# Two small VectorE operations, the clamp of the sums of squares and the layer norms' epsilon, are done on GpSimd beside its powers

## The reference, cut to what matters

```
x = x + 0.5 * ffn(layernorm(x))
x = x + attention(layernorm(x))          # 16 heads of 8, causal
x = x + 0.5 * ffn(layernorm(x))

def ffn(x):                              # 2 layers, 8 heads of 64, window 64
    for l in range(2):
        h = shift_token(x);  q, k, v = split(h @ wqkv[l])
        q = q / max(|q|, 1e-12) * q_scale;  k = k / max(|k|, 1e-12) * k_scale
        q, k = rotary_xpos(q, k)
        x = x + local_attention(q, k, v) @ wo[l]
        h = shift_token(x);  h = (h - mean) / sqrt(var + 1e-5) * ln_g + ln_b
        a, g = split(h @ w1[l] + b1[l]);  x = x + (a * gelu(g)) @ w2[l] + b2[l]
```

## Time and profile before

| | |
|---|---|
| median of 3 runs | 2004.96 us (2004.87 to 2005.1) |
| the profiled execution's own time | 2005.93 us |
| its span in the trace | 2004.1 us |
| busy: PE, DVE, ACT, POOL | 1722.5, 1670.6, 1584.0, 1202.8 us |
| granted TensorE clock, mean | 0.963 of full speed |
| HBM read and written | 5.91 and 2.10 MB |

### The profile page before, as it was taken

One profiled execution on the slowest core, in us unless ns is written; L12 is line 12 of the kernel. 1 busy time (PEld: TensorE's weight loads), 2 busy tenths in 40 slices (PEclk: granted clock), 3 DMA queues, 4 the chain that ended last, 5 costly groups with the idle time before them and its releaser, 6 DMA issues.

```text
span 2004.1 us, 48536 instructions
## 1 busy us (share of the span) xinstructions
PE 1722.5 (86%) x17528; PEld 1353.8 (68%) x17528; DVE 1670.6 (83%) x3487; ACT 1584.0 (79%) x4960; POOL 1202.8 (60%) x1162
## 2 busy tenths in 40 slices
PE   3688999898788899888888889988878889988986
PEld 2477776677667676677766777667766767666775
DVE  6688887888888887888899887888988897888884
ACT  2468897878786899888877789888868778988874
POOL 7677304687678801577788850366767791066870
PEclk7799998999999999999999999999999999999998
DMA  3100000010110000000011000000100010000000
GB/s 100 25 20 12 10 1 17 10 23 20 25 28 20 18 1 3 15 18 18 23 33 25 18 9 1 9 17 17 23 17 23 17 26 2 1 17 18 18 18 11
DMA packets 31686, 36.29 MB, mean 18 GB/s; under 512 B 7986, under 2 KB 18652, under 8 KB 31452
## 3 DMA queue, kind: packets, MB, share of 16 engines
q1 hardware_dynamic: 31452, 33.19, 7.2%
HBM read 5.91 MB, written 2.10 MB: 4 GB/s over the span
## 4 chain that ended last, share of the span: by engine, by line
DVE 36%; ACT 28%; PE 17%; issue 10%; POOL 9%; DMA 0%; ACTq 0%; POOLq 0%; DVEq 0%
ACT probs L885 13%; DVE parts L1152 10%; PE ps_pool L1224 5%; DVE sums L1157 5%; DVE probs L1073 5%; ACT turned L903 4%; POOL rnorm L821 3%; DVE neg_max L1060 3%; PE ps_pool L1297 3%; POOL parts L818 3%; POOL roped L827 3%; ACT L885 2%; ACT L950 2%; DVE sums_floor L1160 2%; PE ps_pool L1368 2%
## 5 line engine op out<-in xcount | busy, mean ns | idle before, releaser
L885 ACT ACTIVATE probs<-ps_scores,neg_max 128x128 f32<-128x128 f32 (+1 forms) x1536 | 577.5, 412 | 71.6 <-DVE neg_max L1060 70.0
L818 POOL TENSOR_TENSOR parts<-parts 128x256 f32<-128x256 f32 x512 | 392.1, 787 | 331.1 <-DVE parts L1152 331.1
L821 POOL TENSOR_TENSOR rnorm<-sums_floor,neg_half 128x8 f32<-128x8 f32 x256 | 440.3, 1720 | 0.0
L885 ACT ACTIVATION_READ_ACCUMULATOR probs<-ps_scores,neg_max 128x1 f32 x1536 | 358.5, 234 | 0.0
L1152 DVE TENSOR_TENSOR parts<-ps_pool,rope 128x1024 f32<-128x1024 f32 x256 | 311.5, 1217 | 38.6 <-ACT squares L931 33.0
L806 POOL TENSOR_TENSOR rstd<-var_eps,neg_half 128x2 f32<-128x2 f32 x112 | 82.0, 732 | 416.8 <-DVE var_eps L1088 413.6
L1060 DVE TENSOR_REDUCE neg_max<-ps_scores 128x4 f32<-128x512 f32 (+1 forms) x448 | 295.4, 682 | 27.5 <-PE ps_scores L1265 16.7
L827 POOL TENSOR_TENSOR roped<-parts,rnorm 128x512 f32<-128x512 f32 x256 | 294.9, 1152 | 37.2 <-POOL rnorm L821 0.9
L1297 PE MATMUL ps_pool<-ident,probs 128*128 128x128 f32 x1792 | 265.7, 286 | 56.0 <-DVE probs L1073 34.8
L903 ACT ACTIVATE turned<-ps_pool 128x512 f32<-128x512 f32 x448 | 255.6, 617 | 63.9 <-PE ps_pool L1297 62.9
L1073 DVE TENSOR_TENSOR probs<-probs,prob_inv 128x1024 f32<-128x1024 f32 (+1 forms) x256 | 293.2, 1166 | 6.6
(11 more groups left out here) (114 smaller groups left out, 3725.7 us busy)
## 6 DMA issues: line engine op xcount, KB each, us to landing
between<-val SPq DMA_DIRECT2D x192, 128.0 KB, 2.2
x_in<-in_L_attn_x_dram SPq DMA_DIRECT2D x16, 128.0 KB, 2.3
out_dram<-x_sb SPq DMA_DIRECT2D x16, 128.0 KB, 1.8
stage<-in_L_ffn_wqkv_dram SPq DMA_DIRECT2D x2, 768.0 KB, 5.4
stage<-in_L_ffn_w_dram SPq DMA_DIRECT2D x2, 341.0 KB
wo<-in_L_ffn_wo_dram SPq DMA_DIRECT2D x2, 256.0 KB
rope_in<-in_rope_dram SPq DMA_DIRECT2D x1, 256.0 KB, 2.9
w<-in_L_ffn_w_dram SPq DMA_DIRECT2D x2, 128.0 KB
```

Source lines behind the costliest of these rows:

```text
L818: last = nc.gpsimd.tensor_tensor(joined[:, :, dst], joined[:, :, dst], sines[:, :, src], ALU.add)
L821: nc.gpsimd.tensor_tensor(rnorm[:, u], sums_floor[:, u], neg_half[:], ALU.pow).then_inc(sems["pool_step"], 1)
L885: last = nc.scalar.activation(probs[:, u, block:block + wide].rearrange("p b j -> p (b j)"), bank[:, at:at + P * wide], ACT.Exp, bias=neg_ ...
```

## The change

The clamp of a Q step's sums and the addition of epsilon leave DVE and become POOL instructions of the same shape, each just ahead of the power that reads it, with a wait of POOL for its own result between. DVE's wait for its own reduction, and for its own aggregation, go with them, and so does the memset of `var_eps`, which the addition overwrites. `squares_summed` is now raised by the reduction and `var_ready` by the aggregation. The counts in `emits` follow. Orders, banks, buffers and DMAs are unchanged.

```diff
-        "LNH": {"vector_step": 2, "var_ready": 1, "rstd_ready": 1},
-        "LNX": {"vector_step": 2, "var_ready": 1, "rstd_ready": 1},
+        "LNH": {"vector_step": 1, "var_ready": 1, "pool_step": 1, "rstd_ready": 1},
+        "LNX": {"vector_step": 1, "var_ready": 1, "pool_step": 1, "rstd_ready": 1},
...
-        "Q": {"squares_ready": 1, "squares_summed": 1, "rope_parts": 1, "vector_step": 1, "pool_step": 2, "rope_ready": 1},
+        "Q": {"squares_ready": 1, "squares_summed": 1, "rope_parts": 1, "pool_step": 3, "rope_ready": 1},
...
                 pool.wait_ge(sems["var_ready"], count("var_ready", step))
+                nc.gpsimd.tensor_scalar(var_eps[s][:], mean_var[s][:, :, 1], EPS, None, ALU.add).then_inc(sems["pool_step"], 1)
+                pool.wait_ge(sems["pool_step"], count("pool_step", step))
                 nc.gpsimd.tensor_tensor(rstd[s][:], var_eps[s][:], neg_half[:, 0:TILES], ALU.pow).then_inc(sems["rstd_ready"], 1)
...
                 pool.wait_ge(sems["squares_summed"], count("squares_summed", step))
+                nc.gpsimd.tensor_scalar(sums_floor[:, u], sums[:, u], NORM_FLOOR * NORM_FLOOR, None,
+                                        ALU.max).then_inc(sems["pool_step"], 1)
+                pool.wait_ge(sems["pool_step"], count("pool_step", step, 1))
                 nc.gpsimd.tensor_tensor(rnorm[:, u], sums_floor[:, u], neg_half[:], ALU.pow).then_inc(sems["pool_step"], 1)
...
                 last.then_inc(sems["vector_step"], 1)
-                dve.wait_ge(sems["vector_step"], count("vector_step", step, 1))
-
-                nc.vector.memset(var_eps[s][:], 0.0)
+                dve.wait_ge(sems["vector_step"], count("vector_step", step))
+
                 for t in range(TILES):
                     last = nc.vector.bn_aggr(mean_var[s][:, t], bn[s][:, t])
-                last.then_inc(sems["vector_step"], 1)
-                dve.wait_ge(sems["vector_step"], count("vector_step", step))
-                nc.vector.tensor_scalar(var_eps[s][:], mean_var[s][:, :, 1], EPS, None, ALU.add).then_inc(sems["var_ready"], 1)
+                last.then_inc(sems["var_ready"], 1)
...
                     nc.vector.tensor_reduce(sums[:, u], squares[:, square].rearrange("p (h d) -> p h d", d=LOCAL_D), AX,
-                                            ALU.add).then_inc(sems["vector_step"], 1)
-                    dve.wait_ge(sems["vector_step"], count("vector_step", step))
-                    nc.vector.tensor_scalar(sums_floor[:, u], sums[:, u], NORM_FLOOR * NORM_FLOOR, None,
-                                            ALU.max).then_inc(sems["squares_summed"], 1)
+                                            ALU.add).then_inc(sems["squares_summed"], 1)
```

## The result

The changed kernel takes 2093.73 us (median of 4 runs, 2088.8 to 2094.57), against 2005.03 us for the kernel before (4 runs): 1.0425 times as long, with a 95% interval from 1.0389 to 1.046. That is 89 us slower. Slower was forecast, 2017 us, in a range up to 2046; the change cost seven times the 12 us of the forecast, and lies outside the range.

The account below looks back on a forecast made before the run. The prediction took the kernel to be bound by DVE between bursts of joins and by POOL in them. 2005.93 us + 45 (POOL's side) - 33 (DVE's side) = 2018, less 1 for the runs' median: 2017 us, range 1982 to 2046.

Parts of the forecast that it names:

- the price of a step: Each POOL step (clamp or epsilon) becomes 0.35 us longer, operation plus wait for its own result; 129 us over 256 + 112 steps.
- the 125: Fall of DVE's sum in us: 82 from the clamps and 43 from the layer norms, idle time ahead of them included.
- R is the tight one: Of the steps behind POOL's longer join, PE's step R, waiting for `roped`, passes the delay on; POOL's side 45 us.
- the short bursts: Some five a round, four joins back to back, ending 1.4 us later; half absorbed by their Rs' slack, 14 us in all.
- The absorption: Behind a long burst's R, PE's one gap of 0.78 us takes up part of 3.85 us; 3.1 us are kept.
- DVE's relief: Gain from DVE's removed clamps and layer-norm work: half of 76 us kept, 38, less 5 for ACT and PE: 33 us.
- The 76 us: DVE's removed work on the chain: 50 us of clamps and 26 us of layer norms, if nothing else came up behind DVE.
- Rival 1: DVE binds and POOL has room: POOL costs 25 us, DVE brings 50, so 1980 us; chance 0.28.
- Rival 2: The new POOL operation costs as much as a two-input one, 0.57 us: POOL's side 73 us, 2053 us; chance 0.14.
- Rival 3: Removing DVE's operations frees POOL too: POOL's side 30 us, the two sides cancel, 2002 us; chance 0.12.
- the signs: Expected in the profile after, among others: PE's `roped` wait 60 us or more, POOL's chain share 15% or more, burst joins 4.9 us apart.

Follow-up runs that it names:

- e3: Kernel before, with the change's 368 small POOL operations and their waits added on spare tiles, DVE keeping all its work: 2097.78 us, 1.0475.
- n2: Changed kernel, with NORM taking a constant and not waiting for `rstd`: 2089.44 us.
- n3: Changed kernel, with R transposing a constant and not waiting for `roped`: 2085.21 us.
- n4: Changed kernel, with neither NORM waiting for `rstd` nor R for `roped`, POOL's work unchanged: 1965.43 us, 0.9809.
- e4: Kernel before, with clamp and epsilon computed nowhere, POOL keeping its old instructions: 1989.61 us, 0.9929.

## Why the prediction was wrong

- **The direction was right, and the price of a step as a sum.** 0.35 us forecast, 0.33 to 0.37 measured. That is partly luck: the operation was put at 0.18 to 0.2 us and takes 0.27 (0.29 for epsilon) in the mean, the wait at 0.145 us and takes 0.08. So POOL's busy time is 1309.9 us against near 1280. DVE's fell by 82 us, not by 125; near 1550 us was forecast, 1588.8 is measured. The three groups that went held 110.6 us; the other 14 of the 125 were idle time, which can't leave the busy time. Other DVE instructions take longer, too: the product of L1078 1351 ns against 1321 before.
- **"R is the tight one" is the step that failed.** The prediction counted POOL's lateness at the R behind the last join of a burst, once a burst, took PE's gaps and half of the short bursts off, and got 45 us. The runs show 94 (e3). Two things were wrong in that step. The count at R was too small: PE waits for `roped` 94 times and not 26, 141.6 us and not 37.4, and with NORM's gate open R alone still gives 2089 us (n2). And lateness is passed on through NORM as well: `rstd` waits in POOL's queue behind joins, and DVE, at the head of a fixed order, stands still for it, 104 us against 14. That wait was named among those behind the join and given no term; with R's gate open it alone still gives 2085 us (n3). n4 shows that the two together are all.
- **The absorption was read off one gap.** The gap of 0.78 us behind one R was taken for absorption. But each late R or NORM stops an engine on which the other three streams depend. That their delay feeds the next join's start is the likely way, but no run isolates it. What is measured: 94 us came through of the 129 that were forecast for POOL (three quarters), or of the 149 that e3's own rows hold (two thirds), and not 45, a third.
- **DVE's relief was mis-sized,** 33 us kept against 14 (e4) alone and at most 6 beside POOL's load. The 76 us were too many as well: the chain of before holds 155 clamps, but with 33.4 us in all, 0.22 us a clamp, where 0.285 was counted; the long clamps mostly are not on it. And a second path, POOL's, lay within some 14 us of DVE's. A chain tells what sets the end, not how much lies right below.
- Rival 1 (DVE's bound, POOL has room) holds for the epsilon alone: 8 us faster. For the clamp it is refuted. Rival 2's price didn't occur. Rival 3 (POOL freed) isn't seen: the means of the power and of `roped` fell, from 1720 to 1698 ns and from 1152 to 1080, and those of the additions and of `rstd` rose, from 787 to 830 and from 732 to 775; over all of them POOL takes 3 us more.
- Of the signs: PE's wait for `roped` was to be at 60 us or more and is 141.6; POOL's share of the chain 15% or more and is 55%. Both point the right way, and their size says that the stages as a whole had turned, not only their bursts. The joins that follow each other without a pause are 4.90 us apart in the mean, 4.48 before, as forecast: POOL's own pace was right, and what the others made of it was not.

## What to carry to other kernels

Before work is moved to an engine that is busy 60% of the span, look at who waits for it at the head of a fixed order, and price each of these waits, not the tightest one. They do not add up: either of the two gates alone let nearly the whole delay through (2089 and 2085 us of 2094), and only with both open was it gone (1965). The chain of one execution gives a bound for a gain, not for a loss; what lies just below it shows when its work is taken out or added in a run of its own, and both signs should be tried, since the slopes here were 0.1 for less of POOL and 0.5 to 0.8 for more. And an engine's small operation can depend on the phase of a neighbour's long one: a shorter POOL join made this kernel 3% slower.

## What the runs showed of the hardware

- GpSimd's tensor_scalar, one input of 8 columns, takes 242 ns in the median and 269 in the mean in the changed kernel, and 225 and 288 for 2 columns; GpSimd's wait for this result is 0.08 to 0.09 us, against 0.14 behind the power.
- One GpSimd addition over 512 columns with the second input in swapped halves takes 1.28 us in the median, `roped` over as many columns 1.04 us.
- A VectorE clamp of 8 columns, SBUF to SBUF, that is issued during a GpSimd addition ends when that addition does: 0.77 us instead of 0.21 in the rows above, 513 ns in the mean of 256 instead of 285. The Trainium skill ("SBUF — State Buffer", section "SBUF: two separate sides") has GpSimd and VectorE's two-port mode hold a shared pair of ports for a whole instruction; these rows agree in that the clamp ends with the GpSimd instruction; which mode the clamp ran in no row shows. They add that cutting the GpSimd addition in two lets the clamp in about where the first half ends, and the kernel before is 62 us faster so than with one addition.
